# Attention in a fused graph layer: the source score as a 129th column of the projection, added as the bias of ACT's copy

## The reference

```python
x = x + _L0_gnn_ref(_layernorm(x), adj, W, a)      # the part that is changed
x = x + _L0_ffn_ref(_layernorm(x), ...)            # 8 experts, top 2, relu
x = x + _L1_gnn_ref(_layernorm(x), adj, ...)       # three GRU steps
x = x + _L1_ffn_ref(_layernorm(x), ...)            # 16 experts, top 2, gated

def _L0_gnn_ref(input, adj, W, a):
    h = jnp.matmul(input, W)
    s1, s2 = h @ a[:F, 0], h @ a[F:, 0]
    e = s1[:, :, None] + s2[:, None, :]            # source score + target score
    e = jax.nn.leaky_relu(e, negative_slope=0.2)
    e = jnp.where(adj > 0, e, -9e15)
    attention = jax.nn.softmax(e, axis=2)
    return jax.nn.elu(jnp.matmul(attention, h))
```

## Time and profile before

| what | value |
|---|---|
| three runs, us | 1063.26, 1065.92, 1068.35; median 1065.92 |
| the profiled execution | 1067.07 us, of which 1065.3 us are its span |
| busy over the span | PE 89%, PE weight loads 72%, DVE 72%, ACT 52%, POOL 56% |
| granted PE clock over the span | 0.936 of full speed |
| PE busy in tenths, first 10 of 40 slices | 4 6 7 6 9 9 9 9 9 9 |
| PE clock in tenths, the same slices | 9 7 7 6 9 9 9 9 9 9 |
| layer 0 (attention and experts) | the first 411 us |

### The profile page before, as it was taken

The page is one execution under the profiler, slowest core; times in us unless marked ns, Lnnn a source line. Parts: engine busy times, 40 slices in busy tenths (PEclk is TensorE's granted clock), DMA queues, the critical chain, the costliest instruction groups (busy, mean ns, idle before and its releaser), DMA issues. The chain is left out here.

```text
span 1065.3 us, 24158 instructions
## 1 busy us (share of the span) xinstructions
PE 950.3 (89%) x6368; PEld 771.2 (72%) x6369; DVE 766.1 (72%) x2968; ACT 553.1 (52%) x1356; POOL 592.7 (56%) x625
## 2 busy tenths in 40 slices
PE   4676999999999996699999999999966899999970
PEld 3566999999989996355555555556535899999970
DVE  5567888888876663478898988989775555555558
ACT  4655665665553342355565655666524344444455
POOL 2155677777777754101355555555536777666670
PEclk9776999999999998699999999999986999999995
DMA  9611422222222422202303133040012643333349
GB/s 225 223 39 60 101 79 81 76 79 73 81 81 74 123 66 85 80 4 77 92 23 106 37 92 104 26 131 26 31 37 66 137 125 94 94 89 92 89 167 363
DMA packets 101512, 99.36 MB, mean 93 GB/s; under 512 B 32412, under 2 KB 86300, under 8 KB 101148
## 3 DMA queue, kind: packets, MB, share of 16 engines
q1 hardware_dynamic: 84252, 62.83, 21.3%
q0 software_dynamic: 17152, 35.29, 9.5%
HBM read 55.44 MB, written 42.62 MB: 92 GB/s over the span
## 5 line engine op out<-in xcount | busy, mean ns | idle before, releaser
L431 POOL DMA_INDIRECT queue<-rows,slots x256 | 260.4, 1017 | 161.5 <-issue 68.7
L2216 POOL DMA_INDIRECT result<-e_y,e_ids x144 | 144.0, 1000 | 57.2 <-issue 46.7
L1006 POOL DMA_INDIRECT result<-a_y,a_ids x136 | 134.4, 988 | 61.8 <-issue 37.2
L2247 PE MATMUL e_ps_h<-e_xT,e_up_of 128*128 128x128 f32 x1152 | 143.1, 278 | 3.0 <-DVE e_hT L2360 2.9
L2247 PEld LDWEIGHTS e_ps_h<-e_xT,e_up_of 128*128 128x128 f32 x1152 | 136.7, 195 | 3.7 <-issue 3.1
L1532 PEld LDWEIGHTS a_ps_y<-w_sb,a_hT 128*128 128x128 f32 x1088 | 131.2, 192 | 4.1 <-issue 1.3
L1532 PE MATMUL a_ps_y<-w_sb,a_hT 128*128 x1088 | 132.6, 275 | 1.1 <-DVE a_y L1165 1.1
L1516 PE MATMUL a_ps_up<-a_xT,a_up_of 128*128 128x256 f32 x448 | 106.7, 381 | 0.0
L2360 DVE TENSOR_TENSOR e_hT<-e_ps_h,e_gate 128x512 f32<-128x512 f32 x72 | 49.7, 690 | 73.6 <-ACT e_gate L2295 73.5
L2295 ACT ACTIVATE e_gate<-e_ps_h 128x512 f32<-128x512 f32 x72 | 43.0, 597 | 96.9 <-PE e_ps_h L2247 96.9
L1516 PEld LDWEIGHTS a_ps_up<-a_xT,a_up_of 128*128 128x128 f32 x448 | 80.7, 190 | 10.1
(11 more groups left out here) (280 smaller groups left out, 2074.5 us busy)
## 6 DMA issues: line engine op xcount, KB each, us to landing
xq<-queue SPq DMA_DIRECT2D x168, 64.5 KB
g_y<-result SPq DMA_DIRECT2D x20, 512.0 KB, 4.1
xq<-queue SPq DMA_DIRECT2D x56, 129.0 KB
x_res<-x SPq DMA_DIRECT2D x16, 256.0 KB, 3.8
w_sb<-w SPq DMA_DIRECT2D x2, 2048.0 KB, 12.8
queue<-rows,slots POOLq DMA_INDIRECT x256, 2.4
w_sb<-w SPq DMA_DIRECT2D x16, 256.0 KB, 4.0
rows<-result SPq DMA_DIRECT2D x8, 512.0 KB, 7.9
```

The costliest lines, as they stand in the source:

```text
L431: pool.indirect_dma_start(out=queue, out_offset=bass.IndirectOffsetOnAxis(ap=c.slots[q][:, k, t:t + 1], axis=0), in_=c.rows[q][:, k, t, :] ...
L1006: pool.indirect_dma_start(out=c.result0, out_offset=bass.IndirectOffsetOnAxis(ap=ids[slot.k][:, t, :].bitcast(U32), axis=0), in_=y[slot.k] ...
L2216: pool.indirect_dma_start(out=result, out_offset=bass.IndirectOffsetOnAxis(ap=ids[at_down.k][:, t, :].bitcast(U32), axis=0), in_=y[at_down ...
L2247: last = pe.matmul(ps_h[b][:, t, q * P:(q + 1) * P], up_of[at_up.k % 4][:, t, q * P:(q + 1) * P], xT[at_up.k % 4][:, t, :], start=True, st ...
```

## The change

The weights of the projection get one column more: `w_sb` is 128 x 129, and column 0 is W a1, copied there at the start. The projection's four products then give the source score of each token beside its 128 features, into `half_o`, a view of both banks of `ps_o`. The eight source products go. ACT copies the four source scores of each partition to `s1` (`copy_s1`), and copies the score tile in four pieces of 64 columns with `s1` as the bias of each. `project` now does the projection first and the scores after it, and `QX` counts "h s". On ACT in slot 1 the copy of the expert rows (`turn_out`) now comes before the copy of e.

The ranks of later groups go to the free half of the bank of `ps_x`. PE makes them in slot 1 between the up and the down products, after ACT has copied the expert rows of that slot; slot 2 waits for `carried` before it transposes into that bank, and `mix` waits for it no more. On DVE `place` moves behind `relu(at_up)`.

```diff
-        w_sb = sb("w", [D, D])
+        w_sb = sb("w", [D, 1 + D])
-        wa_wide = [sb(f"wa{k}_wide", [D, N]) for k in range(2)]
+        wa_wide = sb("wa_wide", [D, N])
+        s1 = sb("s1", [P, G])
...
-        ps_x, ps_y = (pb(name, [P, 512])[:, 0:DOUBLE] for name in ("ps_x", "ps_y"))
+        bank_x = pb("ps_x", [P, 512])
+        ps_x, ps_y = bank_x[:, 0:DOUBLE], pb("ps_y", [P, 512])[:, 0:DOUBLE]
...
         def ranks_at(s):
-            return ps_y[...] if s + 2 < EARLY else ps_o[:, 1, 0:(G + 1) * E0]
+            return ps_y[...] if s + 2 < EARLY else bank_x[:, DOUBLE:DOUBLE + (G + 1) * E0]
...
+                if at_up:
+                    relu(at_up)
                 if two_back is not None:
                     place(two_back)
-                rest(at_up, at_down)
+                if at_down:
+                    add_bias(at_down)
...
+            def copy_s1(s):
+                wait(act, QX, "h", s)
+                act.activation(halves(s1[:].unsqueeze(2)), half_o[:, :, :, 0:1], ACT.Copy).then_inc(AE.sem, 1)
+
             def copy_e(s):
                 wait(act, QX, "s", s)
-                act.activation(e[:], ps_s[:, 0:G * N].rearrange("p (t n) -> p t n", t=G), ACT.Copy).then_inc(AE.sem, 1)
+                wait(act, AE, "s1", s)
+                for t in range(G):
+                    last = act.activation(e[:, t, :], ps_s[:, t * N:(t + 1) * N], ACT.Identity, bias=s1[:, t:t + 1])
+                last.then_inc(AE.sem, 1)
...
             def project(s):
                 pe.wait_ge(turned_out, turn_of["x", s] + 1)
+                wait(pe, VU, "z", s - 1)
+                if s >= EARLY:
+                    wait(pe, VS, "scores", s - 2)
+                for t in range(G):
+                    last = pe.matmul(half_o[:, t // 2, t % 2, :], xnT[:, t * P:(t + 1) * P], w_sb[:],
+                                     start=True, stop=True)
+                last.then_inc(QX.sem, 1)
                 wait(pe, VM, "neg", s)
                 wait(pe, AE, "e", s - 1)
                 for q in range(2):
-                    pe.matmul(ps_s[q * N:(q + 1) * N, 0:G * N], wa_wide[1][:],
+                    pe.matmul(ps_s[q * N:(q + 1) * N, 0:G * N], wa_wide[:],
...
-                for q in range(2):
-                    for t in range(G):
-                        pe.matmul(ps_s[q * N:(q + 1) * N, t * N:(t + 1) * N],
-                                  xnT[:, t * P + q * N:t * P + (q + 1) * N], wa_wide[0][:], start=False, stop=False)
...
-            def expert_slot(now, at_up, at_down):
+            def expert_slot(now, at_up, at_down, ranks_of=None, placed=None):
                 if now:
+                    if placed is not None:
+                        wait(pe, VK, "carried", placed)
...
+                if ranks_of is not None:
+                    pe.wait_ge(xT_copied, now.p + 1)
+                    rank_rows(ranks_of)
                 if at_down:
...
-                if two_back is not None:
-                    rank_rows(two_back)
-                expert_slot(*stages(T, 1))
+                expert_slot(*stages(T, 1), ranks_of=two_back)
...
-                expert_slot(*stages(T, 2))
+                expert_slot(*stages(T, 2), placed=two_back)
```

More of the change, by code:

```diff
@@ L932, in _ @@
             load(0)
-            for dst, src in ((wT_sb[:], gat_wT), (a2_sb[:], gat_a2), (w_sb[:], gat_w), (gw_sb[:], gate_w),
+            for dst, src in ((wT_sb[:], gat_wT), (a2_sb[:], gat_a2), (w_sb[:, 1:], gat_w), (gw_sb[:], gate_w),
                              (gb_sb[:], gate_b.partition_broadcast(P))):
@@ L1034, in copy_products @@
                 v.wait_ge(wa_made, 1)
-                for k in range(2):
-                    last = v.tensor_copy(wa_wide[k][:], ps_t[:, k:k + 1].to_broadcast([D, N]))
-                last.then_inc(wa_copied, 1)
+                v.tensor_copy(w_sb[:, 0:1], ps_t[:, 0:1])
+                v.tensor_copy(wa_wide[:], ps_t[:, 1:2].to_broadcast([D, N])).then_inc(wa_copied, 1)
             def stats(m, V, s):
@@ L1320, in copy_h @@
                 wait(act, QA, "mixed", s - 2)
-                act.activation(h[s % 2][:, :, 0:D], ps_h.rearrange("p (t d) -> p t d", t=G), ACT.Copy,
-                               bias=-1.0).then_inc(AH.sem, 1)
+                act.activation(halves(h[s % 2][:, :, 0:D]), half_o[:, :, :, 1:], ACT.Copy, bias=-1.0).then_inc(AH.sem, 1)
             def exps(s):
@@ L1384, in _ @@
                 if g is not None:
-                    copy_e(g)
+                    copy_s1(g)
                 if now:
@@ L1388, in _ @@
                 if g is not None:
+                    copy_e(g)
                     copy_h(g)
@@ L1456, in project @@
                 pe.wait_ge(turned_out, turn_of["x", s] + 1)
-                wait(pe, VM, "neg", s)
-                wait(pe, AE, "e", s - 1)
-                for q in range(2):
-                    pe.matmul(ps_s[q * N:(q + 1) * N, 0:G * N], wa_wide[1][:],
-                              xnT[:].rearrange("p (t q n) -> p t q n", t=G, q=2)[:, :, q, :], start=True, stop=False)
-                for q in range(2):
-                    for t in range(G):
-                        pe.matmul(ps_s[q * N:(q + 1) * N, t * N:(t + 1) * N],
-                                  xnT[:, t * P + q * N:t * P + (q + 1) * N], wa_wide[0][:], start=False, stop=False)
-                pe.matmul(ps_s[:, 0:G * N], ident_b[:], neg[s % 2][:].rearrange("p t n -> p (t n)"),
-                          start=False, stop=True).then_inc(QX.sem, 1)
                 wait(pe, VU, "z", s - 1)
@@ L1471, in project @@
                 for t in range(G):
-                    last = pe.matmul(ps_h[:, t * D:(t + 1) * D], xnT[:, t * P:(t + 1) * P], w_sb[:],
+                    last = pe.matmul(half_o[:, t // 2, t % 2, :], xnT[:, t * P:(t + 1) * P], w_sb[:],
                                      start=True, stop=True)
                 last.then_inc(QX.sem, 1)
+                wait(pe, VM, "neg", s)
+                wait(pe, AE, "e", s - 1)
+                for q in range(2):
+                    pe.matmul(ps_s[q * N:(q + 1) * N, 0:G * N], wa_wide[:],
+                              xnT[:].rearrange("p (t q n) -> p t q n", t=G, q=2)[:, :, q, :], start=True, stop=False)
+                pe.matmul(ps_s[:, 0:G * N], ident_b[:], neg[s % 2][:].rearrange("p t n -> p (t n)"),
+                          start=False, stop=True).then_inc(QX.sem, 1)
             def rank_rows(s):
@@ L1489, in mix @@
                 wait(pe, AH, "h", s)
-                if s >= EARLY:
-                    wait(pe, VK, "carried", s - 2)
                 for t in range(G):
```

7 lines of the change are left out of this document (4 added, 3 removed).

## The result

| kernel | median us (runs) | ratio to before, 95% interval | profiled: us, of it span |
|---|---|---|---|
| before | 1066.97 (5) | 1 | 1067.07, 1065.3 |
| after | 1072.64 (5) | 1.0056 [1.0041, 1.0071] | 1072.92, 1071.2 |

The change makes the kernel slower by 5.7 us, 0.56%. The forecast was 1068.6 us in a range of 1062.5 to 1075: the time lies in the range and the sign is the one forecast, but the loss is about twice the 2.7 us of the sum. (Of the 4.0 us between 1068.6 and 1072.64, 1.05 come from the median of before, which was 1065.92 over three runs and is 1066.97 over five.) A second comparison with other runs, in experiment 6, gave 1.0046 [1.0026, 1.0066].

A forecast was written before the change was run, and what follows sets the result against it. Early turns were held bound by a single-file chain of waits, dense turns by matmuls, then by ACT's queue. +5.0 early, -0.5 turn 6, -1.8 dense give +2.7 on 1065.92: 1068.6 us, range 1062.5 to 1075.

The forecast's parts named there:

- its first reading: Turns 7 to 15: PE busy without a gap, 188.00 of 188.00 us, so the matmuls set the time.
- its later one: Turns 7 to 15 after the change: PE waits for ACT's queue behind DVE's aggregate; only DVE's 0.13 us are gained.
- The 129th column and PE's saving: Projection's extra column free; dropping eight source products takes 0.84 us off PE per turn, up to 7.6 in dense turns.
- e in four pieces: ACT's copy of the score tile takes 0.95 us instead of 0.37; bounds 0.68 and 1.11.
- Rival (c): ACT's four biased score pieces take 1.65 us instead of 0.95: total +13.2 us, 1079.1; chance 0.08.
- The early term: Turns 0 to 5: score tile 0.83 us later on a single-file chain, +5.0 us; bounds 3.4 and 5.9.
- The wait for the projection: Early turns: projection ahead of scores (0.90 us) is covered by ACT's late arrival; only turn 0 loses some 0.1 us.
- rival (d): Early turns: PE's clock may rise elsewhere, 3 us either way on top of the forecast; no separate chance given.
- Turn 6: The turn between the early and dense kinds: 0.5 us saved, between nothing and 1.5.
- Dense turns: Turns 7 to 15: 0.2 us saved in each, 1.8 us in all; bounds 0.4 and 4.2.
- (a): PE doesn't wait for ACT's queue, so each dense turn saves 0.84 us: -3.1 us, 1062.8; chance 0.10.
- (b): Dense turns save 7.6 us and the score copy is off the early chain: 1057.8; within the 0.07 for faster.

The follow-up runs named there:

- experiment 6: The changed kernel, unedited, run once more beside the kernel before: 1070.23 us, ratio 1.0046.
- experiment 1: The changed kernel with turns 0 to 5 given back their eight source products, single score-tile copy and old order: 1064.92 us, ratio 0.9978.
- experiments 2: The changed kernel with the score tile copied in eight pieces of 32 columns instead of four of 64: 1082.24 us, ratio 1.0151.
- experiment 3: The changed kernel with DVE's statistics of the second normalisation moved ahead of attend, from turn 6 on: 1071.57 us, ratio 1.0042.
- Experiment 9: The changed kernel with turns 0 to 5 as before the change, except the score tile copied in four pieces with zero bias: 1067.9 us, ratio 1.0009.
- experiment 4: The kernel before with only the move of the ranks (bank, place in slot 1, wait for carry, DVE's order): 1068.04 us, ratio 1.0015.

## Why the prediction was right, and where it was not

**What bounds the kernel.** Right on the early turns: undoing them removed the whole loss (experiment 1). On the dense turns its first reading, that "there the matmuls set the time", didn't hold for the changed kernel, and its later one did, that PE would wait for ACT's queue behind the aggregate: PE's full count of busy time hid a chain through ACT and DVE (experiments 2 and 3). That PE shows no idle time was no proof: the end of a matmul is modelled, and a wait of 0.27 between the mix and the next transposes appears only in start to start.

**The 129th column and PE's saving.** "Cost: nothing" came out nearly so: eight records take 0.98 to the next product at the upper level (185.72 to 186.70), for the 0.90 of the earlier trace rows ahead of a much smaller rank product. But the wide scores take 0.59 to the mask for the 0.48 assumed. So of the 0.84 us that "leaves PE", 0.65 left it; how much of the 0.19 is the column and how much the order of the products no run separates.

**e in four pieces.** Forecast 0.95, measured 0.92 to 0.93, pieces of 307 to 334 ns:

```profile
L1326 ACT ACTIVATE a_e<-a_ps_s,a_s x64: 307/316/334, 16.0 to 291.9; 128x64 f32<-128x64 f32 x64
```

By the page on ACT ("ScalarE: Activation LUTs", "What ACT_TABLE_LOAD costs", in the Trainium skill) a piece would be 332 ns and e 1.05; the runs have 316 and 0.92. Rival (c), dear pieces, fell with this. The copy of the source score took 0.15 to 0.17 for the 0.21 assumed.

**The early term is the step that failed in size.** "6 x 0.83 = 5.0 us"; it measured 6.0. Taken from one start of `project` to the next, turns 0 to 5 lost 1.23, 1.27, 0.46, 1.50, 0.90 and 0.64 us. Most of that spread comes from PE's clock just ahead of the start: the four transposes there took 1.09 for 0.63 to 0.65 us, or the reverse. Taken at e, most of it is gone. From ACT's first instruction on e to DVE's it is 1.20 or 1.21 us in turns 1, 2, 3 and 5, for 0.39 or 0.40 before: 0.81 later, and the sum had 0.83. From where DVE takes e in one turn to where it takes it in the next, 0.80, 1.27, 0.81, 0.94 and 0.77 us were lost, behind the 1.24 by which e is late in turn 0.

Two terms that the sum had small or at nothing make the difference of 1.0:

- *The wait for the projection.* The forecast was "this is covered by ACT's late arrival, except in turn 0, where it adds some 0.1", with 0.90 for the projection, the price of a dense turn. At the lower clock level it takes 2.01. In turn 0 ACT starts the pieces 0.69 later than it started the single copy (16.03 for 15.34), and e is 1.24 late instead of about 0.93; in turn 4 the wait adds 0.15.
- *The clock*, which the sum had at nothing and rival (d) allowed 3 us for. The transposes of turn 1's probabilities ran at the lower level behind a wait of 3.62 us, where they had run at the upper one behind 1.92. That is the 1.27, 0.45 above its neighbours:

```profile
30.39 0.66 PE L1440 MATMUL a_ps_t<-ident,a_pbd 128*128 128x128 f32 x4 [1.92 <-ACT a_pbd L1331]
```

```profile
32.43 1.11 PE L1452 MATMUL a_ps_t<-ident,a_pbd 128*128 128x128 f32 x4 [3.62 <-ACT a_pbd L1341]
```

The part of the clock is the weaker one: kernels with the same early code start turn 6 up to 1.4 us apart (94.89 to 96.32), so in other executions it can be more or less. Experiment 9 shows the same loss by parts: 3.1 us for the pieces and 2.3 for the rest.

**Turn 6.** Forecast -0.5, measured -0.22.

**Dense turns.** Forecast -0.2 a turn, measured -0.18 (20.64 for 20.82), 1.4 us over the eight turns between the starts of turns 7 and 15, and nothing after them, for the 1.8 forecast from nine. The aggregate was to end 8.10 after the start and ended 8.15. The place of the wait was one step off: I put it before the up products of slot 3, behind ACT's expert activation. The new wait, 0.27, lies before the transposes of the normalised rows, which come out of the same ACT queue just ahead of it; before slot 3 PE stands 0.10 longer than in experiment 3, but it did so before the change too (0.32 from the expert rows' transposes to the up products in both, 0.22 in experiment 3).

**Rivals (a) and (b)**, PE pays out, fell: 20.58, not 19.9. With the statistics off the path (experiment 3) PE reached 20.10 and not 19.93. That the total came out slower by about what was forecast owes something to luck: the smaller saving on PE could not show, since PE waited in any case.

**Ranks.** Forecast at nothing, 0.05 us a turn at the most (experiment 4).

**Sum.** +6.0 - 0.2 - 1.4 = +4.3 (with two digits: 5.99 - 0.22 - 1.43) at the products ahead of layer 1, against +2.7. Of the 1.6 between them 1.0 is the early term, 0.3 turn 6 and 0.4 the dense turns. The first comparison of medians has +5.7, the second +3.4; layer 1, where one kernel's executions differ by 3.1, can account for what lies between these and 4.3.

## What to carry to other kernels

A product saved on the matmul engine is worth what stands last in its turn, and where turns are of two kinds it has to be asked twice: here the same edit gained 0.2 us in each dense turn and lost 1.0 in each early one, because it put 0.8 us of copies (0.56 for the pieces, 0.25 for the source score) on an engine that was on the path in both. Before an edit frees an engine, count the next one: the queue of POOL, which the prediction had found wide enough for a turn of 20.5 us, took most of the gain at 20.1 until its order was changed. And where a stage is a single file of waits, time each step at the clock level it has there, not at that of the busy stage.

## What the runs showed of the hardware

**POOL's pace.** In layer 0 POOL's indirect DMAs of 128 rows start no closer than 1.25 to 1.26 us, 0.96 of work and 0.30 of issue, in all kernels here. Sixteen a turn are a bound of 20.2 us that no share of busy time shows: POOL counts as 75% busy in experiment 3 (150.92 of 200 us from 130 to 330), where after one wait of 2.98 us at 132.44 it stands no more than 0.31 before any of them.

**Unused products pay.** Three products of 128x512 in a gap of PE brought the transposes, scores and mix behind them from the lower clock level to the upper (0.66, 0.96 and 1.16 us for 1.07, 1.72 and 2.07 in turn 4). Over six turns, with one to six such products in each, it was 5.3 us in one kernel and 4.2 in another.

**The cost of cutting a copy.** On ACT, from PSUM with a bias, 256 columns cost 0.92 in four pieces and 1.53 in eight, 0.15 us for each further piece. From the single copy without a bias (0.37) to four pieces it was 0.18 each.
